# Normalising five blocks of the last stage inside the attention, and loading two adjacency rows one stage ahead

## The reference, cut to what matters

```python
# layer 1, graph part
h = nodes @ weight
logits = (h @ conv_weight1) + (h @ conv_weight2).T
coefs = softmax(leaky_relu(logits, 0.2) + adj, axis=-1)
x = x + coefs @ h + bias

# layer 1, attention and feed-forward part (nh = 4 heads, d = 64, ne = 4 experts)
sx = einsum('bsh,ndh->bnsd', x, hl_w) + hl_b
...                                   # four experts' causal attention, gated and summed: mixed
hn = layernorm(mixed + resid, ln_g, ln_b)
fx = hn, laid out as (tokens, nh, d)
pm = fx == 0
hx = relu(where(pm, 0, fx @ fc1_w.T + fc1_b))
hx = where(pm, 0, hx @ fc2_w.T + fc2_b)
hx = layernorm(hx + fx, fnorm_g, fnorm_b)
fg = softmax(fout @ fgate_w.T, axis=-1)      # fout is hx, laid out as (tokens, 256)
x = x + fout * fg per head
```

## Time and profile before

| | us |
| --- | --- |
| median of 3 runs | 3293.67 (3292.46 to 3295.69) |
| time of the profiled execution | 3291.56 |
| its span, first to last instruction | 3289.8 |
| PE busy | 2946.1 (90%) |
| DVE busy | 1934.4 (59%) |
| POOL busy | 1728.1 (53%) |
| ACT busy | 1255.6 (38%) |

### The profile page before, as it was taken

How to read it: one execution, slowest core, us unless ns; L and a number is a source line. 1 busy time by engine, 2 the same in 40 slices (tenths; PEclk the granted TensorE clock), 3 DMA queues, 4 the chain that set the end, 5 groups by cost and what they waited for, 6 DMA issues and landing times. The chain is left out here.

```text
span 3289.8 us, 45640 instructions
## 1 busy us (share of the span) xinstructions
PE 2946.1 (90%) x17338; PEld 1824.7 (55%) x17338; DVE 1934.4 (59%) x3686; ACT 1255.6 (38%) x1714; POOL 1728.1 (53%) x946
## 2 busy tenths in 40 slices
PE   7999897859999799999999999878999999999953
PEld 3457565548887455555555555445555555555532
DVE  3555664387762466666565662156666566575566
ACT  2242221255553233444444444323434444444423
POOL 0030020233330256778889899735687879888014
PEclk9999887979999799999999999889999999999976
DMA  9971200099990000000000000000000000000001
GB/s 391 423 263 49 64 1 0 35 293 277 270 214 17 3 1 1 1 1 1 1 1 1 1 4 1 1 1 1 1 1 1 1 1 1 1 1 1 1 9 35
DMA packets 63623, 195.20 MB, mean 59 GB/s; under 512 B 8243, under 2 KB 25009, under 8 KB 53426
## 3 DMA queue, kind: packets, MB, share of 16 engines
q1 hardware_dynamic: 38658, 147.98, 11.7%
q0 software_dynamic: 24752, 44.31, 7.5%
HBM read 188.86 MB, written 3.41 MB: 58 GB/s over the span
## 5 line engine op out<-in xcount | busy, mean ns | idle before, releaser
L2136 POOL TENSOR_TENSOR at_acc<-at_acc,at_pt 128x1024 f32<-128x1024 f32 (+1 forms) x628 | 1335.0, 2126 | 233.6 <-ACT at_pt L1879 161.5
L1879 ACT ACTIVATE at_pt<-at_psR 128x1024 f32<-128x1024 f32 (+3 forms) x776 | 700.4, 942 | 936.5 <-PE at_psR L1786 584.2
L1953 DVE TENSOR_REDUCE at_mx<-at_psR 128x2 f32<-128x1024 f32 x576 | 701.6, 1224 | 413.9 <-PE at_psR L1770 411.9
L1804 PE MATMUL at_psO<-at_pt,v 128*64 128x512 f32 (+3 forms) x3104 | 701.6, 573 | 0.4 <-ACT at_pt L1879 0.3
L1770 PE MATMUL at_psR<-at_khi,at_qhi 64*128 64x512 f32 (+3 forms) x1568 | 350.6, 443 | 53.1 <-DVE at_mx L1953 25.5
L1804 PEld LDWEIGHTS at_psO<-at_pt,v 128*64 128x64 f32 x3104 | 191.1, 138 | 328.2 <-issue 227.6
L1770 PEld LDWEIGHTS at_psR<-at_khi,at_qhi 64*128 64x128 f32 x1568 | 154.7, 187 | 326.8 <-issue 296.0
L1783 PE MATMUL at_psR<-at_qhi,at_klo 64*128 64x512 f32 (+2 forms) x1552 | 311.2, 395 | 24.5 <-ACT at_pt L1879 14.5
L1316 PE MATMUL ga_acc<-h,ga_ring 128*128 128x257 f32 (+1 forms) x1352 | 306.9, 388 | 28.9 <-ACT ga_ring L1210 25.2
L1316 PEld LDWEIGHTS ga_acc<-h,ga_ring 128*128 128x128 f32 (+1 forms) x1352 | 259.5, 194 | 74.5 <-ACT ga_ring L1210 32.9
L1783 PE MATMUL at_psR<-at_qlo,at_khi 64*128 64x512 f32 (+2 forms) x1552 | 295.7, 375 | 0.0
(11 more groups left out here) (338 smaller groups left out, 3618.0 us busy)
## 6 DMA issues: line engine op xcount, KB each, us to landing
gc_rows<-in_adj SPq DMA_DIRECT2D x26, 1664.0 KB, 17.4
ga_rows<-in_adj SPq DMA_DIRECT2D x26, 1664.0 KB, 10.3
ga_ring<-in_adjT POOLq DMA_DIRECT2D x78, 512.0 KB, 23.7
gc_cols<-in_adjT SPq DMA_DIRECT2D x26, 1024.0 KB, 14.8
gc_ring<-in_adjT SPq DMA_DIRECT2D x26, 512.0 KB, 8.0
gc_ring<-in_adjT SPq DMA_DIRECT2D x13, 256.0 KB, 2.8
ga_ring<-in_adjT POOLq DMA_DIRECT2D x13, 256.0 KB, 11.1
out_x<-X SPq DMA_DIRECT2D x6, 512.0 KB
```

The costliest lines, as they stand in the source:

```text
L1804: ins = pe.matmul(columns(psO[lanes[l], :], g), v1[:, t, (2 * hp + l) * D:(2 * hp + l + 1) * D], packed(pt[:, g % PTS, l, 0:w], g), start= ...
L1879: act.activation(pt[:, g % PTS, :, 0:w], psR[:, slot_of["score", g] % SLOTS, :, 0:w], ACT.Exp).then_inc(e_ready, 1)
L1953: dve.tensor_reduce(mx[:, u % 2, :, s, c:c + 1].rearrange("p l o -> p (l o)"), got[:, :, 0:w], AX.X, ALU.max).then_inc(p1_read, 1)
L2136: pool.tensor_tensor(to, to, got, ALU.add).then_inc(added, 1)
```

## The change

1. `ga_rows` and its two semaphores move into a new class `GatRows`, opened in `mg`. The SP stream of `stage_gat_prepare` issues the loads of row tiles 0 and 1 behind its own four; the SP stream of `stage_gat` begins with row tile 2.
2. `ff_rstd1` moves into `FfnWeights`, which already lives through attention and last stage. In the last two units of the attention DVE runs one piece of `normalise_early` after the additions of each step: at step 0 variance plus epsilon for the 20 tiles of blocks 0 to 4, at step 4 the reciprocal, at steps 5 to 14 the two operations of each of the five blocks (steps are counted through both units, 13 in each). ACT takes the square root in unit 50 at the end of step 2.
3. In the last stage only the six tiles of blocks 5 and 6 are left for `rstd1`, and only `norm(5)` and `norm(6)` are left, at their old places. PE's `turn` waits on `normed` from block 5 on.

`FfnWeights` and `stage_ffn` also move ahead of the attention in the file, which changes no instruction.

```diff
+class GatRows:
+    def __init__(self, m):
+        self.rows = m.sb("ga_rows", [P, 2, NP])
+        self.loaded = [m.sem(f"ga_rows_loaded{k}") for k in range(2)]
+
+    def load(self, sp, adj, i):
+        b, s = ROW_TILES[i]
+        t = GAT_BLOCKS[b][0] // P + s
+        sp.dma_start(self.rows[:, i % 2, :], adj[t * P:(t + 1) * P, :]).then_inc(self.loaded[i % 2], 16)
...
 def stage_gat_prepare(...):
                 sp.dma_start(b_sb[:, :], row_on_all(bias)).then_inc(w_loaded, 16)
+                for i in range(2):
+                    gat_rows.load(sp, adj, i)
...
 def stage_gat(...):
-                for i, (b, s) in enumerate(ROW_TILES):
-                    if i >= 2:
-                        sp.wait_ge(row_max, i - 1)
-                    t = BLOCKS[b][0] // P + s
-                    sp.dma_start(rows[:, i % 2, :], adj[t * P:(t + 1) * P, :]).then_inc(rows_loaded[i % 2], 16)
+                for i in range(2, len(ROW_TILES)):
+                    sp.wait_ge(row_max, i - 1)
+                    gat_rows.load(sp, adj, i)
...
+EARLY_NORMS = NB - 1
...
 def stage_attention(...):
+        early, er = EARLY_NORMS * SUB, EARLY_NORMS * SUB * NH
...
                         for x in gate_pieces(u, k):
                             gate(*x)
+                        if u == NU - 2 and k == 2:
+                            act.wait_ge(ffn_var, 1)
+                            act.activation(ffn.rstd[:, 0:er], ffn.rstd[:, 0:er], ACT.Sqrt).then_inc(ffn_std, 1)
...
+                def normalise_early(step):
+                    rstd = ffn.rstd[:, 0:er]
+                    if step == 0:
+                        dve.tensor_scalar(rstd, hn_mv[:, 0:early, :, 1].rearrange("p t n -> p (t n)"), EPS2, None,
+                                          ALU.add).then_inc(ffn_var, 1)
+                    elif step == 4:
+                        dve.wait_ge(ffn_std, 1)
+                        link(dve.reciprocal(rstd, rstd))
+                    elif 5 <= step < 5 + 2 * EARLY_NORMS:
+                        b, scaling = divmod(step - 5, 2)
+                        v = hn[:, b * SUB:(b + 1) * SUB, :].rearrange("p t (n d) -> p (t n) d", d=D)
+                        by = (ffn.rstd[:, b * SUB * NH:(b + 1) * SUB * NH] if scaling else
+                              hn_mv[:, b * SUB:(b + 1) * SUB, :, 0].rearrange("p t n -> p (t n)"))
+                        link(dve.tensor_tensor(v, v, by.unsqueeze(2).broadcast_to([P, SUB * NH, D]),
+                                               ALU.mult if scaling else ALU.subtract))
...
                         if u >= LAST_POOL:
                             add_up(FIRST[u] + 2 * k)
                             add_up(FIRST[u] + 2 * k + 1)
+                            normalise_early((u - NU + 2) * steps_of(u) + k)
...
 def stage_ffn(...):
-                    pe.wait_ge(normed, b + 1)
+                    if b >= EARLY_NORMS:
+                        pe.wait_ge(normed, b - EARLY_NORMS + 1)
...
-                act.activation(rstd1[:, :], rstd1[:, :], ACT.Sqrt).then_inc(std1_ready, 1)
+                act.activation(rstd1[:, R0:], rstd1[:, R0:], ACT.Sqrt).then_inc(std1_ready, 1)
...
-                norm(0)
-                norm(1)
                 for b in range(NBLK):
                     mask_hidden(b)
-                    if b + 2 < NBLK:
+                    if EARLY_NORMS <= b + 2 < NBLK:
                         norm(b + 2)
...
 def two_layers(nc, io, out):
+            gat_rows = GatRows(mg)
```

More of the change, by code:

```diff
@@ L1020, with stage_gat_prepare @@
 SLOPE = 0.2
-def stage_gat_prepare(nc, X, mv2, h1, f1_all, f2_all, f1c, f28, f20, ident, all_ones, weight, weightT, conv12, bias):
+def stage_gat_prepare(nc, X, mv2, h1, f1_all, f2_all, f1c, f28, f20, ident, all_ones, gat_rows, adj, weight, weightT, conv12, bias):
     with ExitStack() as ctx:
@@ L1122, in _, with stage_gat @@
                     act.activation((f1_all, f2_all)[z][:, c0:c0 + w], psF[:, n % 2, 0:w], ACT.Copy).then_inc(f_read, 1)
-def stage_gat(nc, X, mv3, h1, f1_all, f2_all, f1c, f28, f20, ident, ones, adj, adjT):
+GAT_BLOCKS = [(NB * BLK, TAIL)] + [(b * BLK, BLK) for b in range(NB)]
+ROW_TILES = [(b, s) for b in range(len(GAT_BLOCKS)) for s in range(GAT_BLOCKS[b][1] // P)]
+class GatRows:
[6 more added lines that the diff above has]
+        sp.dma_start(self.rows[:, i % 2, :], adj[t * P:(t + 1) * P, :]).then_inc(self.loaded[i % 2], 16)
+def stage_gat(nc, X, mv3, h1, f1_all, f2_all, f1c, f28, f20, ident, ones, gat_rows, adj, adjT):
     PAIRS = NT // 2
-    BLOCKS = [(NB * BLK, TAIL)] + [(b * BLK, BLK) for b in range(NB)]
+    BLOCKS = GAT_BLOCKS
     NBK = len(BLOCKS)
@@ L1132, in stage_gat @@
     BANKS = 7
-    ROW_TILES = [(b, s) for b in range(NBK) for s in range(BLOCKS[b][1] // P)]
     ROW_OF = {x: i for i, x in enumerate(ROW_TILES)}
@@ L1137, in stage_gat @@
         ring = m.sb("ga_ring", [P, PAIRS, 2, BLK])
-        rows = m.sb("ga_rows", [P, 2, NP])
+        rows, rows_loaded = gat_rows.rows, gat_rows.loaded
         leaky = m.sb("ga_leaky", [P, 2, NP])
@@ L1147, in stage_gat @@
         psM = m.ps("ga_psM", [P, BLK])
-        rows_loaded = [m.sem(f"ga_rows_loaded{k}") for k in range(2)]
         pair_added = [m.sem(f"ga_pair_added{k}") for k in range(PAIRS)]
@@ L1440, in _, with __init__, load @@
                 tokens(len(blocks) - 1)
+EARLY_NORMS = NB - 1
+class FfnWeights:
+    def __init__(self, m):
+        GW = 2 * NH
+        self.fc1 = m.sb("ff_fc1", [P, P])
+        self.fc2 = m.sb("ff_fc2", [P, P])
+        self.b1 = m.sb("ff_b1", [P, 1])
+        self.b2 = m.sb("ff_b2", [P, 1])
+        self.lng = m.sb("ff_lng", [P, 1])
+        self.lnb = m.sb("ff_lnb", [P, 1])
+        self.fngT = m.sb("ff_fngT", [P, 1])
+        self.fnbT = m.sb("ff_fnbT", [P, 1])
+        self.fgw = m.sb("ff_fgw", [P, DC, NH])
+        self.fgw2 = m.sb("ff_fgw2", [P, DC, GW])
+        self.rstd = m.sb("ff_rstd1", [P, NT * NH])
+        self.loaded = m.sem("ff_w_loaded")
+    def load(self, sp, io):
+        for dst, src in ((self.fc1[:, :], io["fc1"]), (self.fc2[:, :], io["fc2"]), (self.b1[:, :], io["fc1_b"]),
+                         (self.b2[:, :], io["fc2_b"]), (self.lng[:, :], io["ln_g"]), (self.lnb[:, :], io["ln_b"]),
+                         (self.fngT[:, :], io["fnorm_gT"]), (self.fnbT[:, :], io["fnorm_bT"]),
+                         (self.fgw[:, :, :], io["fgate"].rearrange("(c p) n -> p c n", p=P)),
+                         (self.fgw2[:, :, :], io["fgate2"].rearrange("c p n -> p c n"))):
+            sp.dma_start(dst, src).then_inc(self.loaded, 16)
@@ L2167, in _ @@
                             weigh(*x)
-class FfnWeights:
-    def __init__(self, m):
-        GW = 2 * NH
-        self.fc1 = m.sb("ff_fc1", [P, P])
-        self.fc2 = m.sb("ff_fc2", [P, P])
-        self.b1 = m.sb("ff_b1", [P, 1])
-        self.b2 = m.sb("ff_b2", [P, 1])
-        self.lng = m.sb("ff_lng", [P, 1])
-        self.lnb = m.sb("ff_lnb", [P, 1])
-        self.fngT = m.sb("ff_fngT", [P, 1])
-        self.fnbT = m.sb("ff_fnbT", [P, 1])
-        self.fgw = m.sb("ff_fgw", [P, DC, NH])
-        self.fgw2 = m.sb("ff_fgw2", [P, DC, GW])
-        self.loaded = m.sem("ff_w_loaded")
-    def load(self, sp, io):
-        for dst, src in ((self.fc1[:, :], io["fc1"]), (self.fc2[:, :], io["fc2"]), (self.b1[:, :], io["fc1_b"]),
-                         (self.b2[:, :], io["fc2_b"]), (self.lng[:, :], io["ln_g"]), (self.lnb[:, :], io["ln_b"]),
-                         (self.fngT[:, :], io["fnorm_gT"]), (self.fnbT[:, :], io["fnorm_bT"]),
-                         (self.fgw[:, :, :], io["fgate"].rearrange("(c p) n -> p c n", p=P)),
-                         (self.fgw2[:, :, :], io["fgate2"].rearrange("c p n -> p c n"))):
-            sp.dma_start(dst, src).then_inc(self.loaded, 16)
@@ L2539, in two_layers @@
             ones = mg.sb("ones", [P, P])
-            stage_gat_prepare(nc, X, mv, h1, f1_all, f2_all, f1c, f28, f20, ident, ones, io["gat_w"], io["gat_wT"],
+            gat_rows = GatRows(mg)
+            stage_gat_prepare(nc, X, mv, h1, f1_all, f2_all, f1c, f28, f20, ident, ones, gat_rows, io["adj"], io["gat_w"], io["gat_wT"],
                               io["gat_conv"], io["gat_b"])
-            stage_gat(nc, X, mv, h1, f1_all, f2_all, f1c, f28, f20, ident, ones, io["adj"], io["adjT"])
+            stage_gat(nc, X, mv, h1, f1_all, f2_all, f1c, f28, f20, ident, ones, gat_rows, io["adj"], io["adjT"])
         hn = m.sb("hn", [P, NT, DM])
```

570 lines of the change are left out of this document (286 added, 284 removed).

## The result

The changed kernel takes 3285.75 us (median of 17 runs, 3280.47 to 3293.81) where the kernel before takes 3293.76 (17 runs, 3285.18 to 3295.69) on the same chips: a ratio of 0.9981, 95% interval 0.9974 to 0.9989. It is faster by 8.0 us by the medians, by 6.3 by the ratio (which isn't that of the medians), and by 3.6 to 8.6 by its interval. The forecast was 3284.7, with a range of 3281.0 to 3289.5. The profiled execution took 3285.6 for a span of 3283.7, which is 6.1 less than the span of before.

What follows compares the result with a forecast made beforehand. PE was taken to bound graph attention and last attention units, an engine chain the last stage. Gains of 3.35 + 0 + 5.6 = 8.95 us from the median 3293.67 gave 3284.7, range 3281.0 to 3289.5.

Steps and rivals of the forecast that it cites:

- Part 1: Graph attention: two rows loaded a stage ahead start it 3.75 us earlier, less 0.4 for an added barrier: 3.35.
- The moved transfers: Loads of the first two rows, 12.5 us, hide in stage_gat_prepare, which runs 64 us with DMA share 0.04.
- Part 2, DVE: Last two attention units: ten normalising operations of 1.22 us fit DVE's holes of 1.36, costing 0.
- stretched rival: DVE's early operations stretch to 3.09 us as beside POOL; PE stands still 12.2 us, time 3297; chance 0.05.
- Part 2, ACT: Unit 50: two table loads and a square root delay ACT's exponential 0.31 us, within 2.73 of slack, costing 0.
- Part 3: Last stage's start: PE's transposes no longer wait, the ff_back transfer comes last; 4.3 us won, between 4.0 and 4.9.
- Part 4, blocks 2 and 3: Last stage, turns 0 and 1: taking out their normalising pairs wins 0, at most 0.4 us for block 3.
- Part 4, block 4: Last stage, turn 2: without its pair beside POOL it falls from 16.34 to 15.0 us; 1.3 won, between 1.0 and 1.7.
- Swallowed start: Rival: transfers limit the graph attention's first third, so its earlier start wins nothing; time 3288.5, chance 0.12.
- Smaller start of the last stage: Rival: something else there comes late, so its start wins 2.5 us in place of 4.3; time 3286.5, chance 0.08.
- Table switch: Rival: ACT's table switches in the attention hold up PE; 3285.0 at 2.66 us a switch, chance 0.03.

Runs made afterwards that it cites:

- e1: Kernel before with only the two adjacency rows loaded a stage ahead, barrier included: 3292.04 us, ratio 0.9987 to the kernel before.
- e7: Changed kernel with one more DVE operation of the same size behind each of the ten early normalising ones: 3295.63 us, ratio 1.0004 to the kernel before.
- e6: Changed kernel with norm(5) and norm(6) at the last stage's start, row semaphores in the outermost Mem, ff_back loaded during the attention: 3286.80 us, ratio 0.9973.
- b_again: Kernel before, unchanged, run once more for its profile: 3291.16 us, a single run.
- e3: Kernel before with two unused semaphores in mg, which add a clearing and a barrier: 3297.93 us, ratio 1.0002 to the kernel before.
- e5: Changed kernel with norm(5) and norm(6) moved from the loop to the last stage's start: 3287.18 us, ratio 0.9978 to the kernel before.
- e4: Changed kernel with only blocks 0 and 1 normalised early, blocks 2 to 4 back in the loop: 3284.69 us over 6 runs, ratio 0.9967.
- e2: Changed kernel with the early row loads undone, the five blocks still normalised in the attention: 3289.17 us, ratio 0.9979 to the kernel before.
- e8: The kernel of e6 once more, unchanged, for its time and a second profile: 3285.26 us, ratio 0.9976 to the kernel before.

## Why the prediction was right, point by point

- **Part 1, 3.35.** Right. The first maximum starts 3.10 us into the stage (forecast 3.07), 3.73 earlier than before. The barrier costs 0.38 to 0.40 (forecast 0.4). Together 3.54 in the changed kernel and 3.66 in e1.
- **The moved transfers are hidden.** Right: no instruction of the stage waits for the first two rows any more.
- **Part 2, DVE.** Right. The operations take 1.22 beside a quiet POOL, the hole leaves 0.23 (forecast 0.1), PE's step stays 3.92. The stretched rival was priced as ten times what exceeds the hole of 1.36, less 5.5 of slack, and decided from 2.8 us an operation. e7 makes it 2.5: by that rule 10 x 1.14 - 5.5 = 5.9 us, measured 7.9 in units 50 and 51. That the two lie near each other is chance. The rule puts the loss at ACT's buffers, where PE lost nothing; it lost 6.0 at `take_out`, whose slack is 1.2 and which the prediction left out, and 1.75 by the low clock after it. The stretch is a real danger, by another path than the one priced.
- **Part 2, ACT.** Right. The exponential that was due 2.54 us behind the end of the turned-out results (at 3044.89 + 2.54 = 3047.43) starts at 3047.79, 0.36 late (forecast 0.31), and PE shows no hole. The Trainium skill's figure (page ScalarE: Activation LUTs, What ACT_TABLE_LOAD costs: about 2.66 us a switch, drain included) doesn't show: from the first load to the exponential, with two switches and a root of 0.27, it is 3047.79 - 3044.91 = 2.88, the sum of the rows.
- **Part 3, 4.3.** Right in mechanism. The constant comes last, as the trace's own releaser says (0.22 of waiting), and e6 shows what is left without it. The product moved by 6.76 - 2.20 = 4.56. The first masking operation, 14.9 us after the stage's start in the kernel before, b_again and e3, comes after 10.3. The term of 4.3 measured 4.6: I had added 0.3 for landing and release, and it was 0.1.
- **More of the start is PE's clock, not the change.** From the stage's start to the first `weigh` it was 37.27 before and in b_again but 36.33 in e3, whose work is that of before, for L2298 took 3.78 in the one and 2.87 in the other. PE ran at 1.2 GHz there (PEclk 0.50) until 3170 in the kernel before, while e3 was back at 2.4 GHz for part of 3165 to 3170 (PEclk 0.84). Both lengths occur with and without the edit: from the first masking to the first `weigh` it is 22.3 in before, b_again and e5, and 21.4 in e1, e3 and all the others. The changed kernel took 31.67. So of the 5.6 between the two first profiles 0.9 are not won by the edit: 36.33 - 31.67 = 4.7.
- **Part 4, blocks 2 and 3: 0.** Right. From the first masking to the first `weigh` it is 21.4 us in e3 and in the changed kernel, and e4, which puts both back, begins its first `weigh` no later.
- **Part 4, block 4: 1.3.** Right in sign, mis-sized: 1.72 in the changed kernel's first profile, in e2 and in e7, and 0.6 in its second profile, on either side of the bounds of 1.0 and 1.7. I read the turn without the pair as a fixed chain of ACT and DVE, 14.97, from a table load 12.64 into the turn; that load comes at 12.02 in the first profile and at 13.38 in the second. The turn is 14.6 at the least, by DVE, and longer by PE's chain when PE's clock is low in it, here up to 15.8, so the term has no single value.
- **The sum.** 8.95 forecast, 10.5 in the traces, 8.0 by the medians and 6.3 by the ratio. The clock terms just named (0.9 and up to 1.1) take the 10.5 down to 8.5 at most. The wander of the attention and of the first stages, several us in a single profile, stands in any difference of two spans, but not in that of two medians to the same degree. What is left between the traces and the times isn't explained. It isn't this pair's alone: in e6 and e8 the same two stretches are 12.9 and 12.2 us shorter than before, and the times only 7.0 by the medians and 8.9 and 7.9 by the ratios. So that the median fell within 1.1 us of the forecast is in part luck: terms too small (part 3, block 4 in the first profile) stand against up to 4 us that no profile here accounts for. That stays open.
- **The rivals.** Swallowed start: out by e1. Smaller start of the last stage: out by the trace. Stretched operations: out by the trace; e7 shows that they would cost, by `take_out` and not by ACT's buffers. Table switch: out by the trace.

## What to carry to other kernels

Before a wait or a pair of operations is taken out of a loop, ask which engine sets the turn once it is gone, and how fast that engine runs there: here the turn fell from DVE's fixed 16.34 to anything from 14.6 to 16.0, by PE's clock, and the gain was 0.3 to 1.7 from the same edit. When work is slipped into an engine's holes, its cover is the least slack of all that stands behind it in that queue, not only of the buffer nearest to it: 1.2 us at `take_out` here, 5 at the buffers. And compare two spans only after the stretches that both kernels share have been compared: the attention differed by up to 9 us between profiles of the same work here, more than the terms in question.
